# Second expert mixture: answers scattered to their tokens' rows, and the last stage reading whole sequences

## The reference, cut to what matters

```python
x1 = _layernorm(x + attn_out, g1, be1)
gate_probs = jax.nn.softmax(x1 @ Wg + bg, axis=-1)
topk_p, topk_i = jax.lax.top_k(gate_probs, K)                  # K = 2 of E = 8
topk_p = topk_p / jnp.sum(topk_p, axis=-1, keepdims=True)
comb = jnp.sum(jax.nn.one_hot(topk_i, E, dtype=x.dtype) * topk_p[..., None], axis=-2)
h = jax.nn.gelu(jnp.einsum('bsd,edf->bsef', x1, W1) + b1, approximate=False)
y = jnp.einsum('bsef,efd->bsed', h, W2) + b2
moe_out = jnp.einsum('bse,bsed->bsd', comb, y)
return _layernorm(x1 + moe_out, g2, be2)                       # the caller adds x
```

## Time and profile before

| what | value |
| --- | --- |
| median of three runs | 2621.07 us |
| the profiled execution | 2596.13 us, span 2594.0 us |
| busy PE, DVE, ACT, POOL | 2041.2, 2003.5, 1503.4, 567.4 us |
| first gather of the second mixture starts | 2328.98 us |
| last `y_out` of the second mixture starts | 2475.81 us |
| first fetch of the last stage starts | 2479.30 us |

### The profile page before, as it was taken

How to read it: one execution, slowest core, us unless ns; L and a number is a source line. 1 busy time by engine, 2 the same in 40 slices (tenths; PEclk the granted TensorE clock), 3 DMA queues, 4 the chain that set the end, 5 groups by cost and what they waited for, 6 DMA issues and landing times. The chain is left out here.

```text
span 2594.0 us, 46050 instructions
## 1 busy us (share of the span) xinstructions
PE 2041.2 (79%) x16904; PEld 963.5 (37%) x16904; DVE 2003.5 (77%) x3416; ACT 1503.4 (58%) x2914; POOL 567.4 (22%) x692
## 2 busy tenths in 40 slices
PE   6889883694449999999999669999999998359910
PEld 5678663673212222222222322222222222259910
DVE  6676765766678999999996689999999993576635
ACT  3434431142125998989889317998989897105510
POOL 2232220275630000000000250000000000006555
PEclk9999995697677999999999769999999999559955
DMA  4000001035360101111000250110110100302211
GB/s 187 1 0 0 0 0 40 27 98 95 92 184 16 32 24 37 31 30 32 23 23 11 92 165 19 30 41 20 32 42 19 41 6 15 110 7 72 66 50 55
DMA packets 94392, 120.92 MB, mean 47 GB/s; under 512 B 23664, under 2 KB 56560, under 8 KB 93936
## 3 DMA queue, kind: packets, MB, share of 16 engines
q1 hardware_dynamic: 73712, 78.92, 10.9%
q0 software_dynamic: 8960, 18.37, 3.0%
q10 hardware_dynamic: 11520, 20.98, 2.6%
HBM read 69.70 MB, written 42.99 MB: 43 GB/s over the span
## 5 line engine op out<-in xcount | busy, mean ns | idle before, releaser
L1274 DVE TENSOR_REDUCE mx<-psum 128x1 f32<-128x1024 f32 x1024 | 1174.6, 1215 | 79.0 <-PE psum L1162 78.1
L1251 ACT ACTIVATE p<-psum 128x512 f32<-128x512 f32 x2048 | 1102.3, 596 | 107.5 <-PE psum L1184 65.0
L1196 PE MATMUL psum<-p,v_ext 128*32 128x256 f32 x8192 | 655.6, 392 | 39.3 <-ACT p L1251 39.3
L1162 PE MATMUL psum<-ks,qs 64*128 64x512 bf16 x2048 | 635.2, 394 | 52.5 <-DVE mx L1274 30.1
L1184 PE MATMUL psum<-qs,ks 64*128 64x512 bf16 x2048 | 629.8, 383 | 1.4 <-ACT p L1251 1.2
L1196 PEld LDWEIGHTS psum<-p,v_ext 128*32 128x32 f32 x8192 | 161.9, 108 | 473.7 <-ACT p L1251 254.9
L1184 PEld LDWEIGHTS psum<-qs,ks 64*128 64x128 bf16 x2048 | 123.5, 93 | 403.3 <-ACT p L1251 367.3
L1064 POOL CAST m_near<-mx 128x16 bf16<-128x16 f32 x128 | 25.1, 196 | 1080.5 <-DVE mx L1274 1076.3
L605 ACT ACTIVATE hid<-psum,stage 128x128 f32<-128x128 f32 x448 | 132.1, 366 | 180.6 <-PE psum L575 180.6
L549 POOL DMA_INDIRECT x_in<-n_rows,token_of x152 | 166.8, 1098 | 250.3 <-POOLq L85 183.2
L1162 PEld LDWEIGHTS psum<-ks,qs 64*128 64x128 bf16 x2048 | 118.7, 94 | 114.5 <-DVE mx L1274 81.3
(11 more groups left out here) (192 smaller groups left out, 2108.4 us busy)
## 6 DMA issues: line engine op xcount, KB each, us to landing
qs<-qk_parts SPq DMA_DIRECT2D x128, 104.0 KB
ks<-qk_parts SPq DMA_DIRECT2D x128, 104.0 KB
qk_parts<-piece__1 ACTq DMA_DIRECT2D x40, 256.0 KB, 3.7
qk_parts<-piece__2 ACTq DMA_DIRECT2D x40, 256.0 KB, 3.3
answers<-y_out SPq DMA_DIRECT2D x152, 64.0 KB, 1.6
ew<-in_moe SPq DMA_DIRECT2D x1, 5136.0 KB, 19.2
ew<-in_moe SPq DMA_DIRECT2D x1, 4624.0 KB, 14.7
n_rows<-xn SPq DMA_DIRECT2D x8, 512.0 KB, 3.2
```

The lines of the kernel that those rows point to most:

```text
L1162: pe.matmul(psum[:, bank, :], a["qs"][r, g % NKF, j % KM, i * P:(i + 1) * P], a["ks"][r, g % NKF, j % KM, k * HALF:(k + 1) * HALF], start= ...
L1196: last = pe.matmul(psum[GR * j:GR * j + VW, O_BANK, q], t["v_ext"][:, b * NT + i, VE * (h0 + j):VE * (h0 + j) + VW], a["p"][:, (GH * s + j ...
L1251: act.activation(a["p"][:, n % NP, :], psum[:, S_BANK + n % NS, :], ACT.Exp, scale=DH ** -0.5)\
L1274: dve.tensor_reduce(a["mx"][:, g % 2, h, j, 0, c:c + 1], psum[:, bank:bank + 2, :].rearrange("p a c -> p (a c)"), AX.X, ALU.max)\
```

## The change

In the second mixture each slot now knows its pair (token and choice), from which follow the token (`token_of`) and a row of a new DRAM tensor `pair_answers` (`place_of`). That tensor holds the first choices of all tokens, then the second choices, then spare rows for slots without a pair. The tile's answers are scattered there by an indirect DMA on GpSimd, five tiles behind the gather; SyncE's stores to `answers` are gone in this layer. The last stage loads whole sequences by SyncE with two plain DMAs each, and the gain, the shift and the sum with x are done on GpSimd by halves of a sequence. The normalised values have two buffers (`x2`, `x2_b`).

```diff
 def invert(nc, t, layer, tiles):
-                                      flat(hi)[:, n:n + 1], t["token"][:, n // 2:n // 2 + 1],
+                                      flat(hi)[:, n:n + 1], t["token"][:, n:n + 1],
...
-            link(dve.tensor_scalar(t["token_f"][:, 0:tiles], psum[:, 2, 0:tiles], -1.0, 0.0, ALU.add, ALU.max))
-            dve.tensor_copy(t["token_of"][:, 0:tiles], t["token_f"][:, 0:tiles])
+            link(dve.tensor_copy(of, psum[:, 2, 0:tiles]))
+            link(dve.tensor_scalar(token, of, B * L + 0.5, -float(B * L), ALU.is_gt, ALU.mult))
+            link(dve.scalar_tensor_tensor(token, token, -1.0, of, ALU.add, ALU.add))
+            dve.tensor_scalar(t["token_of"][:, 0:tiles], token, 0.0, None, ALU.max)
+            if layer:
+                link(dve.scalar_tensor_tensor(place, of, 0.0, t["spare"][:, 0:tiles], ALU.is_equal, ALU.mult))
+                dve.scalar_tensor_tensor(t["place_of"][:, 0:tiles], place, -1.0, of, ALU.add, ALU.add)
...
 def expert_tiles(nc, t, layer, tiles, F, func):
+    NX, NST, AHEAD = PLACES, 3, 5
...
+            def scatter(i):
+                pool.wait_ge(y_ready, i + 1)
+                pool.indirect_dma_start(t["pair_answers"],
+                                        bass.IndirectOffsetOnAxis(ap=t["place_of"][:, i:i + 1], axis=0),
+                                        t["y_out"][:, i % NX, :], None).then_inc(stored[i % NX], 16)
+
+            for i in range(tiles + AHEAD):
+                if i < tiles:
+                    gather(i)
+                if layer and i >= AHEAD:
+                    scatter(i - AHEAD)
+            if layer:
+                for i in range(tiles - NX, tiles):
+                    pool.wait_ge(stored[i % NX], 16 * (i // NX + 1))
+
+        if not layer:
+            @block.sync
...
 def finish(nc, t, x, n):
+            def load(b):
+                if b >= 2:
+                    sp.wait_ge(mixed, 2 * NT * (b - 1))
+                for k in range(2):
+                    r = B * L * k + L * b
+                    sp.dma_start(t["back"][:, b % 2, k, :, :], t["pair_answers"][r:r + L, :].rearrange("(i p) d -> p i d", p=P))\
+                        .then_inc(loaded[b % 2], 16)
+
+            load(0)
+            load(1)
             for b in range(B):
                 for h in range(NH):
                     sp.wait_ge(added, NH * b + h + 1)
...
+                if b + 2 < B:
+                    load(b + 2)
...
-                if b >= 2:
-                    pool.wait_ge(mixed, 2 * NT * (b - 1))
-                fetch(pool, t, b)
+                for h in range(NH):
...
+                    pool.wait_ge(normed, NT * b + TPH * (h + 1))
+                    pool.tensor_tensor(x2[b % 2][:, s, :], x2[b % 2][:, s, :], row("g2"), ALU.mult).then_inc(scaled, 1)
+                    pool.wait_ge(scaled, n)
+                    pool.tensor_tensor(x2[b % 2][:, s, :], x2[b % 2][:, s, :], row("be2"), ALU.add).then_inc(shifted, 1)
+                    pool.wait_ge(shifted, n)
+                    pool.tensor_tensor(x[b](h * TPH, TPH), x[b](h * TPH, TPH), x2[b % 2][:, s, :], ALU.add)\
+                        .then_inc(added, 1)
...
-                link(dve.tensor_tensor(x2[:, :, :], x2[:, :, :], t["row"]("g2"), ALU.mult))
-                link(dve.tensor_tensor(x2[:, :, :], x2[:, :, :], t["row"]("be2"), ALU.add))
-                for h in range(NH):
-                    dve.tensor_tensor(x[b](h * TPH, TPH), x[b](h * TPH, TPH), x2[:, h * TPH:(h + 1) * TPH, :],
-                                      ALU.add).then_inc(added, 1)
```

More of the change, by code:

```diff
@@ L490, in floor, with invert @@
     link(dve.tensor_scalar(x, x, -float(3 * 2 ** 22), None, ALU.add))
-def invert(nc, t, tiles):
+def invert(nc, t, layer, tiles):
     psum, T = t["psum"], B * NT
@@ L529, in _, with expert_tiles @@
                 last.then_inc(used, 1)
-def expert_tiles(nc, t, tiles, F, func):
+def expert_tiles(nc, t, layer, tiles, F, func):
     psum, W1, W2, B1 = t["psum"], 0, F * P, 2 * F * P
     B2 = B1 + F
-    NX, NST = PLACES, 3
+    NX, NST, AHEAD = PLACES, 3, 5
     with stage(nc, "staged", "turned", "x_ready", "hidden", "activated", "y_done", "y_ready",
@@ L545, in _, with gather @@
         def _(pool):
-            for i in range(tiles):
+            def gather(i):
                 if i >= NX:
@@ L551, in _ @@
                     .then_inc(gathered[i % NX], 16)
[L553 to L559, removed]
+            def scatter(i):
[13 more added lines that the diff above has]
+            @block.sync
+            def _(sp):
+                for i in range(tiles):
+                    sp.wait_ge(y_ready, i + 1)
+                    sp.dma_start(t["answers"][i * P:(i + 1) * P, :], t["y_out"][:, i % NX, :])\
+                        .then_inc(stored[i % NX], 16)
+                for i in range(tiles - NX, tiles):
+                    sp.wait_ge(stored[i % NX], 16 * (i // NX + 1))
         @block.tensor
@@ L709, in finish @@
 def finish(nc, t, x, n):
-    xn, x2 = t["xn"], t["x2"]
-    with stage(nc, "mixed", "step", "var_ready", "std_ready", "normed", "added") as \
-            (block, mixed, step, var_ready, std_ready, normed, added):
+    xn, x2 = t["xn"], (t["x2"], t["x2_b"])
+    with stage(nc, "mixed", "step", "var_ready", "std_ready", "normed", "scaled", "shifted", "added",
+               "loaded0", "loaded1") as \
+            (block, mixed, step, var_ready, std_ready, normed, scaled, shifted, added, *loaded):
         @block.sync
         def _(sp):
+            def load(b):
[7 more added lines that the diff above has]
+            load(1)
             for b in range(B):
@@ L726, in _ @@
             for b in range(B):
-                if b >= 2:
-                    pool.wait_ge(mixed, 2 * NT * (b - 1))
-                fetch(pool, t, b)
+                for h in range(NH):
+                    s = slice(h * TPH, (h + 1) * TPH)
+                    row = lambda name: t["row"](name)[:, s, :]
+                    n = NH * b + h + 1
+                    pool.wait_ge(normed, NT * b + TPH * (h + 1))
[5 more added lines that the diff above has]
+                        .then_inc(added, 1)
         @block.scalar
@@ L1420, in mixture @@
                 t["lo_hot"], t["hi_hot"] = sb("lo_hot", [P, 2, INV, P], where=scope), sb("hi_hot", [P, 2 * INV, tiles], where=scope)
-                t["token_f"] = sb("token_f", [P, tiles], where=scope)
-                t["token_of"] = sb("token_of", [P, tiles], U32, where=scope)
+                for name in ("pair_f", "token_f", "place_f"):
+                    t[name] = sb(name, [P, tiles], where=scope)
+                t["token_of"], t["place_of"] = (sb(name, [P, tiles], U32, where=scope) for name in ("token_of", "place_of"))
                 for name in ("x_in", "y_out"):
@@ L1433, in mixture @@
                 route(nc, t, layer, E, tiles)
-                invert(nc, t, tiles)
-                expert_tiles(nc, t, tiles, F, func)
+                invert(nc, t, layer, tiles)
+                expert_tiles(nc, t, layer, tiles, F, func)
         mixture(0, 16, 2, ACT.Relu, 80, lambda b: gate_logits(nc, t, w, 0, b, 16, t["x"]()))
@@ L1477, in build @@
         with ExitStack() as scope:
-            t["back"] = sb("back", [P, 2, NT, 2, D], where=scope)
-            t["mixed"] = sb("mixed", [P, NT, D], where=scope)
+            t["back"] = sb("back", [P, 2, 2, NT, D], where=scope)
+            t["mixed"], t["x2_b"] = (sb(name, [P, NT, D], where=scope) for name in ("mixed", "x2_b"))
             finish(nc, t, [view(x_all, b) for b in range(B)], [view(n_all, b) for b in range(B)])
```

23 lines of the change are left out of this document (17 added, 6 removed).

## The result

The changed kernel takes 2653.31 us in the median (2651.90 to 2656.12) where the kernel before takes 2621.61: a ratio of 1.0122 with an interval of 1.0104 to 1.0139, 32 us slower. The range ended at 2650.

The account below looks back on a forecast made before the run. TensorE bounds the second mixture's tiles, GpSimd's fetches the last stage. Terms 46.7 - 40.3 + 1.5 = +7.9 us gave 2604.0 against the profiled 2596.13; put on the 2621.07 median, 2629.0, range 2606 to 2650.

Parts of the forecast that it names:

- the forecast's +5 to +16: Whole kernel, the favoured case: 17 in place of 13 to 21 us of blocking, 2.65 to 2.75 a tile; 2626 to 2637, chance 0.32.
- put the difference on the median: Whole kernel: the earlier median, 2621.07, lay 25 us above the profiled execution; with the difference added, the forecast was 2629.0.
- Tiles' stage, +46.7: Second mixture's tiles: GpSimd becomes the bound with a gather and a scatter per tile; the stage grows by 46.7 us.
- The price of a pair: Second mixture's tiles: gather plus equally priced scatter take 2.67 us a tile, between 2.50 and 2.85.
- a cover of 4.6 us hides it: Second mixture's tiles: `y_out` is done at 10.0 us, its scatter comes at 14.6, so GpSimd's wait costs nothing.
- Last stage, -40.3: Last stage: plain loads replace GpSimd's 64 fetches; it takes 76.1 us instead of 116.4, shrinking by 40.3.
- C: Last stage: what GpSimd's sums cost VectorE in sequences 1 to 3; taken as 17 us, cases from 1.2 to 21.
- the theory of taking turns: Last stage: GpSimd and VectorE alternate, each sum costing VectorE 1.17 us, 7.0 a sequence, 21 in all.
- `invert`, +1.5: `invert`: two more operations in the first mixture and four in the second, about 0.24 us each and a hop: 1.5 us.
- The engines do block each other: Answers the rival that GpSimd and VectorE hardly block each other: -16 to -9 us, 2605 to 2612, chance 0.28.
- the clock does not fall: Answers the rival that TensorE's clock falls in the tiles' gaps: some 3.8 us a tile, about 2700, chance 0.04.
- The dearer stream: Tiles, rival: GpSimd's mixed stream costs more than its gathers, by 2.17 us late starts or copies; +20 to +25, chance 0.14.

Follow-up runs that it names:

- experiment 4: Changed kernel with the last stage's sums back on VectorE, plus weight copy on ScalarE: ratio 0.9981 in the second mixture alone, 0.9934 (2581.40 us) in both.
- The fastest version: Changed kernel with sums back on VectorE and weight copy on ScalarE in both mixtures, scatters five tiles behind gathers: 2581.40 us, 0.9934 of before.
- variant with lead seven: Changed kernel with sums on VectorE, weight copy on ScalarE in both mixtures, scatters seven tiles behind gathers instead of five: 1.0078 of before, late chip.

## Why the prediction was wrong, step by step

**The number.** Against the kernel before of an on-time chip, from which the profile came, the sum said +7.9 us, and the two spans differ by 2609.3 - 2594.0 = 15.3. As a difference that lies inside the forecast's +5 to +16, with its mechanism; of the 7.4 us to the sum, 4.7 are in the tiles and 2.6 in the last stage. The step that failed is the last one: "I know no cause in the trace, and put the difference on the median". The 25 us between profile and median were the mark of a late chip, on which TensorE's results come late where GpSimd issues indirect transfers back to back: in the first mixture, and at the start of the second. The change makes them back to back through the whole second mixture. So the difference could not be added as a constant. On the late chip the last scatter starts at 2570.15; if it lands 2.25 us later, as on the on-time chip, the tiles' stage takes 222.6 us, 74.0 more than the 148.6 of before, of which 8 belong to before as well: 66 instead of 46.7. Less the last stage's 38, and with the 1.5 of `invert`, that is 30 of the 32 us. That the range was missed by only 3 us is no merit of the sum: its upper part stood for other causes.

**Tiles' stage, +46.7.** On the on-time chip it is 2530.6 - 2330.6 = 200.0 us from the first gather to the last landing, +51.4. The mechanism was right: GpSimd is the bound, a scatter costs a gather, the clock stays at 1.00 with TensorE busy for 150.72 of 192 us, and no stall of 2.17 us came. The price of a pair was 0.055 us too low (2.725 for 2.67), and with the few gaps the pace was 2.735, 4.2 us over 65 tiles, nearly all of the miss. The waits for `y_out` are 3.7 us, 2.3 of them behind the last gather, where the forecast has them too. The step "a cover of 4.6 us hides it" held here; on the late chip the cover was used up (19.3 us of waits).

**Last stage, -40.3.** It measured 78.7 us, -37.7. C, the disputed term, was 17 and is 9.5 us on the combinations plus 12.4 x 3/4 = 9.3 on the normalisations of three sequences, 18.8: near the 21 of the theory of taking turns, since each of six sums holds up one VectorE operation by some 1.05 us. Barrier and first load took 2.6 and 6.05 us for 1.7 and 5.0, and the end behind the last sum 3.2 for 4.0.

**`invert`, +1.5.** The first gather starts at 2330.62, against 2328.98 and 2326.90 in two profiles of before, so these cannot tell the term from the spread.

By the Trainium skill ("SBUF — State Buffer", section "SBUF: two separate sides") GpSimd and VectorE hold a shared pair of ports in turn. The normalisations have one input tile in SBUF and were held up as much as the combinations. The Trainium skill's box in that section, on GpSimd's transfers being held up by VectorE's fp32 copy, agrees with experiment 4, where the copy cost each transfer 0.07 to 0.10 us. The statistics of this stage (278 ns) tell nothing of the turns, since no sum of GpSimd runs beside them: in the last sequence they run from 2593.04 to 2594.68, and the sums before them end at 2589.71. Their one place beside a sum is that of rows 9.

**The rivals.** The engines do block each other, and the clock does not fall on an on-time chip. On the late one it is 0.91 in the mean, and behind the gap of 3.94 us at 2411.84 eight matmuls take 2.08 us where those of 2404.04 took 1.10. The dearer stream had its chance of 0.14 for a time of 2641 to 2646; it came dearer by a mechanism that none of the rivals had.

## What to carry to other kernels

When a profile's own time and the timed runs differ by 1%, find the stage in which they differ before adding up: a constant offset is itself a claim. Look for stretches in which GpSimd issues indirect transfers back to back beside TensorE, since on some chips they hold up its results. And when GpSimd becomes the bound, look at what VectorE does to its instructions: moving the fp32 copy to ScalarE took the ratio from 1.0027 to 0.9981 in one mixture (12 us) and to 0.9934 in both (24 us).

## What was not expected of the hardware

Two kinds of chip: the attention between the mixtures takes the same time on both (from the end of the first mixture's last `y_out` to the second's first gather 1716.7 us on the late one, 1716.5 on the other), and so does the last stage. Only TensorE's results beside dense indirect transfers differ: they come up to 6.45 us late in the changed kernel, and up to 52 us with a gather every 1.25 us that nothing waits for. The Trainium skill ("SBUF — State Buffer", section "SBUF: two separate sides") says that a DMA cannot be slowed by a compute op, and vice versa. The 43 matmuls in 63 us are against it in their effect, but the trace does not tell whether the matmuls themselves or only the signal of their end are late. That stays open, and so does what distinguishes the chips. The fastest version itself did not run on a late chip, only its variant with lead seven.
